# Tile 6 finished between the two halves of tile 7's right product, one correction moved to GpSimd, splits and copies moved

## The reference

```python
x = x + ffn(cond(x, itok, W, lora_A, lora_B), W_base, b_base, W_gate, A, B)

def cond(x, idx, W, lora_A, lora_B):          # x: 8 x 128 x 512
    xr = einsum('bsi,bir->bsr', x, lora_A[idx])
    return einsum('bsi,io->bso', x, W) + einsum('bsr,bro->bso', xr, lora_B[idx])

def ffn(x, W_base, b_base, W_gate, A, B):
    probs = softmax(einsum('bnd,ed->bne', x, W_gate))
    # the two best of 8 experts, their weights divided by their sum: route_w
    h = einsum('bnd,erd->bner', x, A)
    return (einsum('bnd,od->bno', x, W_base) + b_base
            + einsum('bner,eor->bno', h * route_w[..., None], B))
```

## Time and profile before

| | |
|---|---|
| median of 3 runs | 66.23 us (65.94 to 67.05) |
| the profiled execution | 66.37 us, its span 65.2 us |
| TensorE busy | 60.0 us, 92% |
| VectorE busy | 49.9 us, 77% |
| ScalarE busy | 33.9 us, 52% |
| GpSimd busy | 22.9 us, 35%, none of it behind 38.1 us |
| TensorE's granted clock | 1.00 in every slice of the span |

### The profile page before, as it was taken

The page is one execution under the profiler, slowest core; times in us unless marked ns, Lnnn a source line. Parts: engine busy times, 40 slices in busy tenths (PEclk is TensorE's granted clock), DMA queues, the critical chain, the costliest instruction groups (busy, mean ns, idle before and its releaser), DMA issues.

```text
span 65.2 us, 1329 instructions
## 1 busy us (share of the span) xinstructions
PE 60.0 (92%) x406; PEld 58.3 (89%) x406; DVE 49.9 (77%) x155; ACT 33.9 (52%) x91; POOL 22.9 (35%) x45
## 2 busy tenths in 40 slices
PE   4989999999999999999999997999999999999900
PEld 4969999999999999999998995999999997999600
DVE  0957999908799999998888568669766699886800
ACT  2753999315799394452170955478084713452310
POOL 1000799899404994994059930000000000000000
PEclk9999999999999999999999999999999999999999
DMA  0799999404994035323233330810008000034072
GB/s 0 223 339 376 381 398 401 154 3 126 358 329 169 6 96 129 67 61 70 57 78 64 67 79 18 293 49 0 0 9 313 10 0 0 0 134 175 13 263 64
DMA packets 5529, 8.75 MB, mean 134 GB/s; under 512 B 1009, under 2 KB 2065, under 8 KB 5522
## 3 DMA queue, kind: packets, MB, share of 16 engines
q1 hardware_dynamic: 4978, 7.88, 37.4%
q0 software_dynamic: 256, 0.52, 2.3%
q10 hardware_dynamic: 288, 0.27, 1.2%
HBM read 5.26 MB, written 2.10 MB: 113 GB/s over the span
## 4 chain that ended last, share of the span: by engine, by line
PE 78%; DVE 7%; DMA 5%; issue 2%; ACT 2%; DVEq 0%; ACTq 0%
PE bank L809 19%; PE bank L811 18%; PE bank L810 18%; PE bank L817 8%; PE bank L819 5%; DMA w_raw<-fold_in 5%; PE bank L983 3%; PE bank L935 2%; DVE cs_lo L589 2%; PE bank L942 1%; PE bank L987 1%; PE bank L952 1%; PE bank L921 1%; DVE top_diff L735 1%; DVE bank L685 1%
## 5 line engine op out<-in xcount | busy, mean ns | idle before, releaser
L809 PE MATMUL bank<-c_hi,x_hi 128*128 128x408 f32 (+1 forms) x40 | 13.6, 339 | 0.5 <-ACT x_raw L516 0.5
L811 PE MATMUL bank<-c_hi,x_lo 128*128 128x408 f32 (+1 forms) x40 | 13.4, 335 | 0.0
L810 PE MATMUL bank<-c_lo,x_hi 128*128 128x408 f32 (+1 forms) x40 | 13.4, 334 | 0.0
L809 PEld LDWEIGHTS bank<-c_hi,x_hi 128*128 128x128 f32 x40 | 7.5, 188 | 0.8 <-issue 0.8
L589 DVE TENSOR_TENSOR x_lo<-x_raw,x_hi 128x512 fp32r<-128x512 f32 (+1 forms) x10 | 8.0, 824 | 0.0
L810 PEld LDWEIGHTS bank<-c_lo,x_hi 128*128 128x128 f32 x40 | 7.5, 188 | 0.0
L811 PEld LDWEIGHTS bank<-c_hi,x_lo 128*128 128x128 f32 x40 | 7.5, 188 | 0.0
L331 POOL DMA_DIRECT2D lora_raw<-lora x8 | 4.4, 554 | 6.5 <-issue 6.3
L496 ACT ACTIVATE top_exp<-top_diff 128x2 f32<-128x2 f32 x8 | 1.6, 204 | 6.8 <-DVE top_diff L735 6.8
L809 PE MATMUL bank<-ffn_b_hi,hw_hi 128*128 128x256 f32 x16 | 4.9, 305 | 0.0
L811 PE MATMUL bank<-ffn_b_hi,hw_lo 128*128 128x256 f32 x16 | 4.5, 282 | 0.0
(11 more groups left out here) (140 smaller groups left out, 188.7 us busy)
## 6 DMA issues: line engine op xcount, KB each, us to landing
x_raw<-x_t SPq DMA_DIRECT2D x8, 256.0 KB, 4.2
out<-w_raw SPq DMA_DIRECT2D x7, 256.0 KB, 2.2
w_raw<-fold_in SPq DMA_DIRECT2D x4, 256.0 KB, 4.6
w_raw<-fold_in SPq DMA_DIRECT2D x3, 324.0 KB, 4.6
bw_rows<-bw_hi SPq DMA_DIRECT2D x16, 40.5 KB, 2.1
lora_raw<-lora POOLq DMA_DIRECT2D x8, 64.0 KB, 3.3
bw_rows<-bw_lo SPq DMA_DIRECT2D x8, 40.5 KB, 2.1
ffn_b_raw<-ffn_b SPq DMA_DIRECT2D x1, 256.0 KB, 5.7
```

What stands on the lines that cost most here:

```text
L809: nc.tensor.matmul(out, a_hi, b_hi, start=first, stop=False, skip_group_check=True)
L810: nc.tensor.matmul(out, a_hi, b_lo, start=False, stop=False, skip_group_check=True)
L811: return nc.tensor.matmul(out, a_lo, b_hi, start=False, stop=last, skip_group_check=True)
```

## The change

TensorE: `M6(3)` is cut in its two chunks. Tile 6's `Lora_right`, `T2(7)` and `Delta(6)` stand between them, and `T2(6)` moves ahead of `M7(3)`. GpSimd: `sum_u2(3)` moves there from VectorE. ScalarE: `copy_m5(2)` goes ahead of `exp_top(3)`, `exp_top(4)` ahead of `copy_left(2)`, the high part of SUM6 goes forward to SUM7's, and `copy_left(5)` goes behind `split_hw(6)`. VectorE: the low part of SUM7 moves from behind `seed_u(2)` to behind `sum_e(2)`, that of SUM6 from between the two `split_xa` of pair 3 to ahead of `split_hw(4)`. The diff's pieces stand in the order GpSimd, ScalarE, VectorE, TensorE.

```diff
+            def sum_u2(q):
+                k = SEVEN.index(q)
+                pool.wait_ge(z_done, k + 1)
+                pool.wait_ge(hw_done, 2 * q + 2)
+                pool.wait_ge(u1_done, k + 1)
+                nc.gpsimd.tensor_tensor(mix(q)[:, 2], mix(q)[:, 2], mix(q)[:, 0], ALU.add).then_inc(u2_done, 1)
...
             split_la_pair(3)
+            sum_u2(3)
...
             copy_right(1)
+            copy_m5(2)
             exp_top(3)
-            copy_m5(2)
             copy_m4(2)
             split_hw(2)
             split_cs(SUM7, 4)
+            split_cs(SUM6, 1)
...
             copy_xa_t(2)
-            split_cs(SUM6, 1)
+            exp_top(4)
             copy_left(2)
-            exp_top(4)
...
             exp_top(7)
-            copy_left(5)
             copy_right(5)
             split_hw(6)
+            copy_left(5)
...
             sum_e(2)
+            split_cs(SUM7, 2)
             split_xa(4)
...
             gate(5)
+            split_cs(SUM6, 3)
             split_hw(4)
             seed_u(2)
-            split_cs(SUM7, 2)
             sum_e(3)
             split_xa(6)
-            split_cs(SUM6, 3)
             split_xa(7)
...
-            sum_u2(3)
-
+
+            dve.wait_ge(u1_done, len(SEVEN))
             dve.wait_ge(zr_done, NT - 1)
...
             M7(2)
             T1(3)
-            M6(2)
+            M6(2, (0, 1))
...
             Delta(5)
+            T2(6)
             M7(3)
-            T2(6)
-            M6(3)
-            Lora_right(3, (6, 7))
+            M6(3, (0,))
+            Lora_right(3, (6,))
             T2(7)
             Delta(6)
+            M6(3, (1,))
+            Lora_right(3, (7,))
             Delta(7)
```

More of the change, by code:

```diff
@@ L695, in sum_u1 @@
                 nc.vector.tensor_tensor(mix(q)[:, 0], first_bank[:, M1_COLS], mix(q)[:, 0], ALU.add).then_inc(u1_done, 1)
[L697 to L701, removed]
             steps = [0]
@@ L887, in M2, with seven_right @@
                 seven_left(2 * q + 1, 0, C01, q, False).then_inc(left_done, 1)
-            def seven_right(out, q, which, done, seeded):
+            def seven_right(out, q, which, done, seeded, chunks=(0, 1)):
                 pe.wait_ge(xd_lo_done, SEVEN.index(q) + 1)
@@ L892, in seven_right @@
                     pe.wait_ge(cs_lo_done, done)
-                for c in range(2):
+                for c in chunks:
                     mm = product(out, xd_chunk(x_hi, q, which, c), xd_chunk(x_lo, q, which, c),
@@ L905, in M7, with M6 @@
                 seven_right(right(2 * q), q, SUM7, 2, q == SEVEN[0])
-            def M6(q):
+            def M6(q, chunks):
                 pe.wait_ge(yr_done, 2 * q)
-                seven_right(right(2 * q + 1), q, SUM6, 3, q == SEVEN[0])
+                seven_right(right(2 * q + 1), q, SUM6, 3, q == SEVEN[0], chunks)
             def T1(q):
```

## The result

The changed kernel takes 65.61 us in the median of 20 runs (64.79 to 66.29), the kernel before 66.41 (65.66 to 67.06). The ratio is 0.9866 with a 95% interval of 0.9835 to 0.9897: 1.3% faster. 65.33 of 66.23 had been forecast, a ratio of 0.9864. The profiled execution took 65.62 us with a span of 64.4. (Some executions of most kernels fell in a slower state, and the ratios leave them out; the profiled ones of cs_alone, old_tail, u2_dve and best, further down, are such executions.)

What follows compares the result with a forecast made beforehand. TensorE, 78% of the chain that ended last, was taken to bound the kernel through gaps in its starts. 0.20 + 0.37 + 0.21 - 0.03 + 0.15 = 0.90 us gave 65.33 against 66.23; 8-in-10 range 64.6 to 65.9.

Steps and rivals of the forecast that it cites:

- The reading of the gaps: TensorE from 38 us on: gaps of 0.72 behind `T2(2)`, 0.37 at `T1(3)`, 0.21 ahead of `Delta(7)`; together 1.30 us.
- Part 1: `copy_m5(2)` ahead of the exponential: M3(2) 0.72 early, but `T2(3)` then held by `hw_lo` of tile 2; gain 0.20 us.
- Part 2: Both `cs_lo` out of VectorE's queue ahead of `T1(3)`, which then waits for nothing; gain 0.37 us.
- Part 3: TensorE's end: `T2(7)` sooner, so `Delta(7)` no longer waits; gain 0.21 us, less 0.03 for `T2(7)`.
- Part 4: `sum_u2(3)` on GpSimd ends between 59.9 and 60.4, ahead of tile 7's last addition; costs nothing, 0.2 to 0.7 in hand.
- rival (c): GpSimd's sum also holds VectorE's `hw_lo` of tile 7, `Delta(7)` 0.2 late: 65.5 us; chance within the forecast's 0.62.
- rival (d): Slower than before: GpSimd's sum ends last, tile 7's addition pays each microsecond beyond 60.6; 66.7 with 3 us; chance 0.04.
- Part 5: Last stores: tile 6's leaves earlier, so less stands in front of the last; gain 0.15 us, between 0 and 0.7.
- The sum: All parts: 0.20 + 0.37 + 0.21 - 0.03 + 0.15 = 0.90 us, 65.33 against the median of 66.23.
- Rival (a): `T2(3)` isn't held by `hw_lo` of tile 2, or the store gains its full 0.7: 0.5 more, 64.8; chance 0.17.
- Rival (b): A closed gap's time is lost at the next meeting, as at `T1(3)` or `T2(7)`: 0.3 to 0.6 less, 65.8; chance 0.17.

Runs made afterwards that it cites:

- cs_alone: Kernel before with only the SUM7 and SUM6 split moves, on both engines; ratio to before 0.9873, last product 21.32 us behind `T2(2)`.
- old_tail: Changed kernel with TensorE's last stretch back in the order of before (`M6(3)` whole, `T2(6)` behind `M7(3)`); ratio to before 0.9957.
- u2_dve: Changed kernel with `sum_u2(3)` back on VectorE, behind `hw_lo` of tile 7; ratio to before 0.9886.
- best: cs7_late, lr7_early and left_first in one kernel; ratio to before 0.9820, median 65.19 us.
- m5_alone: Kernel before with only `copy_m5(2)` moved ahead of `exp_top(3)`; ratio to before 0.9837.
- cs7_late: Changed kernel with VectorE's low part of SUM7 moved from behind `sum_e(2)` to behind `gate(5)`; ratio to before 0.9758.
- lr7_early: cs7_late with tile 7's `Lora_right` also ahead of `T2(7)`; ratio to before 0.9820.
- left_first: Changed kernel with `Delta(7)` writing its left half first, so ScalarE's store is issued ahead of SyncE's; ratio to before 0.9884.
- u2_dve_again: The kernel of u2_dve run a second time; last product 21.02 us behind `T2(2)`, 3.5 us from it to the end.
- store_sp: Changed kernel with the last store (left half of tile 7) issued by SyncE in place of ScalarE's queue; ratio to before 0.9865.
- gp_three: Changed kernel with two more unused sums of the same size on GpSimd ahead of `sum_u2(3)`; ratio to before 0.9972.

## Why the prediction was right

**The reading of the gaps** held. All three were of the size read from the starts: m5_alone closed the first for 0.74 (0.72 forecast), cs_alone the second for 0.36 (0.37), and the third, 0.21, is gone in the changed kernel.

**Part 1** held in its mechanism: `T2(3)` waits for `hw_lo` of tile 2, behind a `cs_lo` that starts at 41.39 (41.37 forecast). m5_alone, cs7_late and cs_alone show both halves of it: without the subtraction no wait, and without the early copy no cost. The size was 0.19: the first product behind `T2(3)` came 42.93 - 39.84 = 3.09 behind `T2(2)` before and 42.78 - 39.88 = 2.90 after; 0.20 had been forecast. That close a match is partly luck, since errors cancelled: `T2(3)` started 42.73 - 42.58 = 0.15 behind the end of `hw_lo`, not 0.05; the product behind it came 0.05 later, not 0.10; and `T2(2)` itself stood 0.04 later, while `hw_lo` stood where it was.

**Part 2** held: `T1(3)` at 54.00 (53.91 forecast) with no wait. M2(3)'s end came last for `split_xa(7)`, which was over at 53.60 + 0.17 = 53.77 (53.74 forecast). The distance to `T1(3)` fell by 14.57 - 14.12 = 0.45; 0.19 of that are part 1's, and the 0.07 of its slower restart come on top, 0.33 in all against 0.37.

**Part 3** was mis-sized in one term. The wait ahead of `Delta(7)` went for its full 0.21, but that of `T2(7)` for `hw_lo` of tile 6 took 0.16, not 0.03, by the same hand-over: `hw_lo` ended at 58.59 + 0.28 = 58.87, and `T2(7)` started at 59.02. So the cut of `M6(3)` gave 0.05 at the last product by old_tail, and 0.62 - 0.19 - 0.33 = 0.10 by what is left of the whole, where 0.18 had been put down. Parts 1 to 3 together gave 0.62 in place of 0.75. The recorded working also has a slip that changed no term: it puts `Delta(7)` 1.23 behind `T2(7)` (at 60.06), but the second product behind a transposition comes 0.20 after the first (59.08 to 59.28), and `Delta(7)` came 1.32 behind it (59.02 to 60.34). So the margins of part 4 and of the wait for `hw_lo` of tile 7 were 0.09 wider than stated, and rival (c) would have cost 0.1, not 0.2.

**Part 4** held for the changed kernel: 0.74 us on GpSimd, 0.86 in hand, and nothing gained or lost (u2_dve). While GpSimd ran from 59.37 to 60.11, `hw_lo` of tile 7 on VectorE took its usual 0.29 at 59.65, with one operand in a bank. So rival (c) is refuted here. The Trainium skill (SBUF — State Buffer, "SBUF: two separate sides") has it that VectorE contends with GpSimd only with two SBUF inputs or in a two-port mode. By that rule `hw_lo` doesn't wait, and the trace agrees. The price of a late GpSimd, rival (d), stays open.

**Part 5** has about the size that was forecast; its mechanism has support, but no run isolates it. The span shrank by 0.8 where the last product came 0.58 sooner on the same clock, so 0.22 are behind it (3.68 - 3.46), where 0.15 had been forecast. The four kernels with the old end of TensorE's list (before, m5_alone, cs_alone, old_tail) take 3.63 to 3.68 there, the three with the changed kernel's store order and an earlier tile 6 (changed, cs7_late, lr7_early) 3.46 to 3.58. In all seven the last store is issued 0.71 or 0.72 behind the last product, so what shrank is the time that it takes to land. That fits the argument that tile 6's earlier store makes room for the last (0.73 us ahead of it before, 1.02 after). But no run moves tile 6's store alone, and left_first and best, with the two halves in the other order, took 3.6 and 3.8 although tile 6's store was as early: there the last store was issued 0.84 and 0.83 behind the last product and took 2.7 and 2.9 to land.

**The sum** came out because the errors offset each other: parts 1 to 3 gave 0.13 less than forecast, and the stretch behind the last product 0.07 more, 0.84 together in place of 0.90. The profiled executions differ by 0.75 us (66.37 and 65.62), the medians by 0.80. The ratio of 0.9866 against 0.9864 is closer than that, and far closer than the interval, which is 0.4 us wide, can tell. That part of the agreement is luck.

**Rival (a)** described what the change would have given without the misplaced subtraction: 0.5 us more. cs7_late shows 0.56 at the last product. **Rival (b)** came partly true, with the 0.16 ahead of `T2(7)`, but for 0.13 us in place of 0.3 to 0.6.

## What to carry to other kernels

When a gap on the bounding engine is closed, look at what its next waits need and what the same change puts ahead of that on the other engines. Here an operation moved into a gap of VectorE used up the time in which VectorE had waited for the very product that now came sooner. The gap was idle only because of the stall that was being removed. And where executions differ by a shift in their first microseconds, count from a start that the edit doesn't touch.

## What the runs showed of the hardware

The shift of up to 0.97 us in `T2(2)` arises at the very start. TensorE's first four products on the raw weights (one group of eight passes in the timeline) lasted 1.77 us before, and 2.18 in cs_alone, with the same granted clock of 1.00 in that stretch. TensorE's timelines of the kernel before and of cs_alone:

```profile
3.87 1.77 PE L983 MATMUL bank<-w_raw 128*128 128x136 f32 x8 [0.24 <-DMA w_raw<-fold_in]
5.47 1.03 PE L987 MATMUL bank<-w_raw 128*128 128x256 f32 x4
```

```profile
3.86 2.18 PE L983 MATMUL bank<-w_raw 128*128 128x136 f32 x8 [0.23 <-DMA w_raw<-fold_in]
5.83 1.09 PE L987 MATMUL bank<-w_raw 128*128 128x256 f32 x4
```

The same products, released at the same time, and those behind them 0.36 us later; cs_alone's `T2(2)` starts 0.37 later too. The thirteen executions fall in two groups by this: six have 2.18 in the first row, and their `T2(2)` starts at 40.21 or later; seven have 1.45 to 1.84, and theirs starts at 39.88 or sooner. Why the products run at different speeds no run here tells. It makes times spread by 1% and more, as much as the change itself.

`T2` released by `hw_lo` starts 0.15 us behind its shown end (42.58 to 42.73, 58.87 to 59.02), whereas `T1(3)` started 0.05 behind the end of `split_xa(7)` before. Both are transpositions released by VectorE. It isn't `hw_lo` as such, for before, the first product of `Delta(7)`, released by the `hw_lo` of tile 7, started 0.05 behind its end too (60.77 to 60.82). What makes the difference stays open.

Of two stores of 128 KB issued 0.1 to 0.5 us apart, the first landed in 1.7 to 2.2 us and the last mostly in 2.5 to 2.9, whichever queue it was on. The last one's time goes neither with its queue nor with its distance from the other half's store (2.9 at 0.24 us, 2.5 at 0.14 and 0.38), but roughly with how far ahead of it tile 6's store of 256 KB was issued:

| from tile 6's store to the last one, us | kernels | the last one landed in, us |
|---|---|---|
| 0.73 to 0.79 | before, m5_alone, cs_alone, old_tail | 2.9 in each |
| 0.89 to 1.02 | lr7_early, best, changed, cs7_late | 2.9, 2.9, 2.8, 2.7 |
| 1.11 to 1.16 | u2_dve, u2_dve_again, left_first, store_sp | 2.5, 2.6, 2.7, 2.5 |
| 1.35 | gp_three | 2.1 |

This is an order found in thirteen executions, not an experiment on it. It would explain why gp_three, which delayed its last store, ended no later for it.
